# Attention on one Trainium2 core: softmax denominators by ones in both column halves, the output scaled on the vector engine, and one maxima piece between two score groups

## The reference, cut to what matters

```python
q = jnp.einsum('bnsd,neod->bneso', sx, wq)          # 4 heads x 4 experts
k = jnp.einsum('bnsd,nod->bnso', sx, wk)
v = jnp.einsum('bnsd,nod->bnso', sx, wv)
scores = jnp.einsum('bnesd,bntd->bnest', q, k) * d ** 0.5 + causal
att = jax.nn.softmax(scores, axis=-1)
qkv = jnp.einsum('bnest,bntd->bnesd', att, v)
qkv = jnp.where(pad[:, :, None], 0.0, qkv)
out = jnp.transpose(qkv, (0, 1, 3, 2, 4)).reshape(b, nh, s, ne * d)
gs = jax.nn.softmax(jnp.einsum('bnsf,nef->bnse', out, gate_w) + gate_b[None, :, None, :], axis=-1)
mixed = jnp.einsum('bnsed,bnse->bnsd', out.reshape(b, nh, s, ne, d), gs)
```

## Time and profile before

| | |
|---|---|
| median of 3 runs | 3468.97 us (3467.27 to 3474.9) |
| the profiled execution | 3469.29 us, span 3467.6 us |
| busy share of the span | PE 89%, PEld 54%, DVE 51%, ACT 36%, POOL 54% |
| instructions | 46110 |
| mean granted clock of PE | 0.937 |

### The profile page before, as it was taken

How to read it: one execution, slowest core, us unless ns; L and a number is a source line. 1 busy time by engine, 2 the same in 40 slices (tenths; PEclk the granted TensorE clock), 3 DMA queues, 4 the chain that set the end, 5 groups by cost and what they waited for, 6 DMA issues and landing times. The chain is left out here.

```text
span 3467.6 us, 46110 instructions
## 1 busy us (share of the span) xinstructions
PE 3079.7 (89%) x18162; PEld 1862.0 (54%) x18162; DVE 1757.7 (51%) x2797; ACT 1236.7 (36%) x1637; POOL 1862.6 (54%) x992
## 2 busy tenths in 40 slices
PE   7999987689998889999999999788999999999943
PEld 3445656377875555555555555455555555555422
DVE  4522764487833455565555640155656565563056
ACT  2210320356531233334444344233343434434423
POOL 0000020333310356778788899546677879889924
PEclk9999888899998799999999999789999999999966
DMA  9951100399950000000000000000000000000001
GB/s 392 424 207 46 60 1 8 110 295 272 261 94 15 1 1 1 1 1 1 1 1 1 1 1 1 1 1 1 1 1 1 1 1 1 1 1 1 1 4 40
DMA packets 63748, 195.36 MB, mean 56 GB/s; under 512 B 8243, under 2 KB 25137, under 8 KB 53554
## 3 DMA queue, kind: packets, MB, share of 16 engines
q1 hardware_dynamic: 38786, 148.11, 11.1%
q0 software_dynamic: 24752, 44.31, 7.1%
HBM read 188.99 MB, written 3.41 MB: 55 GB/s over the span
## 5 line engine op out<-in xcount | busy, mean ns | idle before, releaser
L1866 POOL TENSOR_TENSOR at_acc<-at_acc,at_pt 128x1024 f32<-128x1024 f32 (+3 forms) x728 | 1556.9, 2139 | 277.9 <-ACT at_pt L1702 194.7
L1762 DVE TENSOR_REDUCE at_mx<-at_psR 128x2 f32<-128x1024 f32 (+3 forms) x784 | 858.6, 1112 | 854.2 <-PE at_psR L1593 539.4
L1702 ACT ACTIVATE at_pt<-at_psR 128x1024 f32<-128x1024 f32 (+3 forms) x784 | 731.1, 936 | 991.5 <-PE at_psR L1614 607.3
L1630 PE MATMUL at_psO<-at_pt,v 128*64 128x512 f32 (+3 forms) x3136 | 702.7, 569 | 15.8 <-DVE at_oT L1781 10.6
L1611 PE MATMUL at_psR<-at_qhi,at_klo 64*128 64x512 f32 (+3 forms) x1568 | 345.9, 436 | 58.7 <-ACT at_pt L1702 27.5
L1630 PEld LDWEIGHTS at_psO<-at_pt,v 128*64 128x64 f32 x3136 | 193.1, 138 | 338.2 <-issue 277.2
L1593 PE MATMUL at_psR<-at_khi,at_qhi 64*128 64x512 f32 (+3 forms) x1568 | 341.9, 430 | 33.7 <-ACT at_pt L1702 9.4
L1246 PE MATMUL ga_acc<-h,ga_ring 128*128 128x257 f32 (+1 forms) x1352 | 305.3, 386 | 29.8 <-ACT ga_ring L1140 26.3
L1611 PEld LDWEIGHTS at_psR<-at_qhi,at_klo 64*128 64x128 f32 x1568 | 152.1, 188 | 328.9 <-issue 306.2
L1611 PE MATMUL at_psR<-at_qlo,at_khi 64*128 64x512 f32 (+3 forms) x1568 | 300.8, 377 | 0.0
L1611 PE MATMUL at_psR<-at_qhi,at_khi 64*128 64x512 f32 (+3 forms) x1568 | 300.1, 376 | 0.0
(11 more groups left out here) (318 smaller groups left out, 3276.8 us busy)
## 6 DMA issues: line engine op xcount, KB each, us to landing
gc_rows<-in_adj SPq DMA_DIRECT2D x26, 1664.0 KB, 17.3
ga_rows<-in_adj SPq DMA_DIRECT2D x26, 1664.0 KB, 9.9
ga_ring<-in_adjT POOLq DMA_DIRECT2D x78, 512.0 KB, 23.7
gc_cols<-in_adjT SPq DMA_DIRECT2D x26, 1024.0 KB, 15.1
gc_ring<-in_adjT SPq DMA_DIRECT2D x26, 512.0 KB, 7.6
gc_ring<-in_adjT SPq DMA_DIRECT2D x13, 256.0 KB, 2.8
ga_ring<-in_adjT POOLq DMA_DIRECT2D x13, 256.0 KB, 9.2
out_x<-X SPq DMA_DIRECT2D x6, 512.0 KB
```

What stands on the lines that cost most here:

```text
L1630: ins = pe.matmul(psO[lanes[l], off:off + w], v1[:, t, (2 * hp + l) * D:(2 * hp + l + 1) * D], pt[:, g % PTS, l, 0:w], start=g == FIRST[u] ...
L1702: act.activation(pt[:, g % PTS, :, 0:w], psR[:, slot_of["score", g] % SLOTS, :, 0:w], ACT.Exp).then_inc(e_ready, 1)
L1762: dve.tensor_reduce(mx[:, u % 2, :, s, c:c + 1].rearrange("p l o -> p (l o)"), psR[:, slot_of["max", i] % SLOTS, :, 0:w], AX.X, ALU.max).t ...
L1866: pool.tensor_tensor(to, to, got, ALU.add).then_inc(added, 1)
```

## The change

The turn `t` no longer makes the denominators. A new turn `d` comes ahead of it: for each head one matmul with a 128x64 block of ones as stationary and all of `acc` (up to 512 columns) as moving operand, into the head's 64 partitions of `psX`, so that each denominator stands in 64 rows. `scale_out` on DVE takes the reciprocal in place in `psX` and multiplies `oT` by it. The turn `t` then waits for `o_scaled`. In a step list `d` stands where the first `t` stood (step 1), the two `t` stand one step later (steps 2 and 3, or the last step if there are fewer). The gate no longer divides. Its pieces come a step later in units of 5 or more steps, and in units of 5 steps pieces 1 and 2 fall into the same step. `max_pieces` keeps the number of pieces of a step but puts at most one after the first score group: (2,1) becomes (1,2), (3,3) becomes (1,5). POOL may start on a reused `acc` after `d` instead of after the last `t`.

```diff
@@ late_turns
-        out += [("t", u - 1, h) for h in range(halves_of(u - 1)) if k == min(1 + h, ls - 1)]
+        if k == min(1, ls - 1):
+            out.append(("d", u - 1))
+        out += [("t", u - 1, h) for h in range(halves_of(u - 1)) if k == min(2 + h, ls - 1)]
@@ max_pieces
-    lo, hi = (len(some) * (2 * k + h) // (2 * steps_of(u)) for h in (half, half + 1))
+    lo, hi = (len(some) * x // steps_of(u) for x in (k, k + 1))
+    between = min(lo + 1, hi)
+    lo, hi = (lo, between) if half == 0 else (between, hi)
@@ gate_pieces
-            return [(hp, b, i) for i in range(3) if k == 2 + i]
+            return [(hp, b, i) for i in range(3) if k == (3 + i if ls >= 6 else min(3 + i, 4))]
@@
-LAST_TURNS = [("t", NU - 1, h) for h in range(halves_of(NU - 1))]
+LAST_TURNS = [("d", NU - 1)] + [("t", NU - 1, h) for h in range(halves_of(NU - 1))]
@@ tensor
+                def denominators(u):
+                    bw = QBLOCKS[UNITS[u][1]][1]
+                    pe.wait_ge(x_read, turn_of["d", u])
+                    pe.wait_ge(added, FIRST[u + 1])
+                    for l in range(2):
+                        ins = pe.matmul(psX[lanes[l], 0:bw], ones_f[:, :], acc[:, u % 2, l, 0:bw], start=True, stop=True)
+                    ins.then_inc(x_full, 1)
+
                 def turn_out(u, h):
                     hp, b, e = UNITS[u]
                     pe.wait_ge(x_read, turn_of["t", u, h])
-                    pe.wait_ge(o_read, u + 1)
-                    pe.wait_ge(added, FIRST[u + 1])
+                    pe.wait_ge(o_scaled, u + 1)
                     for s in range(2 * h, 2 * h + 2):
-                        o = (s - 2 * h) * (TCOLS + 2)
-                        pe.matmul(psX[:, o:o + TCOLS], oT[:, u % 2, s * P:(s + 1) * P], tg_sb[:, hp, e, :],
-                                  start=True, stop=True)
-                        for l in range(2):
-                            ins = pe.matmul(psX[:, o + TCOLS + l:o + TCOLS + l + 1],
-                                            acc[:, u % 2, l, s * P:(s + 1) * P], one[:, :], start=True, stop=True)
+                        o = (s - 2 * h) * TCOLS
+                        ins = pe.matmul(psX[:, o:o + TCOLS], oT[:, u % 2, s * P:(s + 1) * P], tg_sb[:, hp, e, :],
+                                        start=True, stop=True)
                     ins.then_inc(x_full, 1)
@@ vector
+                def scale_out(u):
+                    bw = QBLOCKS[UNITS[u][1]][1]
+                    dve.wait_ge(x_full, turn_of["d", u] + 1)
+                    link(dve.reciprocal(psX[:, 0:bw], psX[:, 0:bw]))
+                    dve.wait_ge(o_read, u + 1)
+                    dve.tensor_tensor(oT[:, u % 2, 0:bw], oT[:, u % 2, 0:bw], psX[:, 0:bw], ALU.mult).then_inc(o_scaled, 1)
+                    dve.wait_ge(o_scaled, u + 1)
+                    dve.sem_inc(x_read, 1)
@@ vector, gate
-                        link(dve.reciprocal(rden[:, 0:ws, :, :].rearrange("p s e l -> p (s e) l"),
-                                            onx[:, 0:ws, :, 2 * NE:2 * NE + 2].rearrange("p s e l -> p (s e) l")))
-                        link(dve.tensor_tensor(
-                            gp[:, 0:ws, :, :].rearrange("p s e (l g) -> p (s e) l g", g=NE),
...
-                        link(dve.tensor_tensor(gates, gates, gate_max.unsqueeze(2).broadcast_to([P, 2 * ws, NE]), ALU.mult))
-                        dve.tensor_tensor(wgt[:, 0:ws, :, :], gs[:, 0:ws, :].rearrange("p s (l g) -> p s g l", l=2),
-                                          rden[:, 0:ws, :, :], ALU.mult).then_inc(gate_ready, 1)
+                        for l in range(2):
+                            ins = dve.tensor_tensor(
+                                wgt[:, 0:ws, :, l], gs[:, 0:ws, l * NE:(l + 1) * NE],
+                                gate_max.rearrange("p (s l) -> p s l", l=2)[:, :, l:l + 1].broadcast_to([P, ws, NE]), ALU.mult)
+                        ins.then_inc(gate_ready, 1)
@@ gpsimd, add_up
                         if u >= 2:
-                            pool.wait_ge(x_full, last_turn(u - 2) + 1)
+                            pool.wait_ge(x_full, turn_of["d", u - 2] + 1)
```

More of the change, by code:

```diff
@@ L1486, in stage_attention @@
         ones_r = m.sb("at_ones_r", [P, P], F32R)
-        one = m.sb("at_one", [P, 1])
+        ones_f = m.sb("at_ones_f", [P, D])
         pt = m.sb("at_pt", [P, PTS, 2, BLK])
@@ L1516, in stage_attention @@
         added = m.sem("at_added")
-        o_read = m.sem("at_o_read")
+        o_read, o_scaled = m.sem("at_o_read"), m.sem("at_o_scaled")
         gate_shifted, gate_exped, gate_ready = m.sem("at_gate_shifted"), m.sem("at_gate_exped"), m.sem("at_gate_ready")
@@ L1571, in turn_out @@
                     pe.wait_ge(x_read, turn_of["t", u, h])
[L1572 to L1573 removed]
+                    pe.wait_ge(o_scaled, u + 1)
                     for s in range(2 * h, 2 * h + 2):
[L1575 to L1580 removed]
+                        o = (s - 2 * h) * TCOLS
+                        ins = pe.matmul(psX[:, o:o + TCOLS], oT[:, u % 2, s * P:(s + 1) * P], tg_sb[:, hp, e, :],
+                                        start=True, stop=True)
                     ins.then_inc(x_full, 1)
                 def turn(kind, *what):
[L1584 removed]
+                    {"k": keys, "q": queries, "r": row_of_maxima, "d": denominators, "t": turn_out}[kind](*what)
                 def row_max(u, i, s, c, w):
@@ L1688, in turn_out @@
                         act.wait_ge(mix_done, block_number(hp, b))
-                    got = psX[:, 0:2 * (TCOLS + 2)].rearrange("p (s c) -> p s c", s=2)
+                    got = psX[:, 0:2 * TCOLS].rearrange("p (s c) -> p s c", s=2)
                     act.activation(on[:, 2 * h:2 * h + 2, e, :], got[:, :, 0:P], ACT.Copy)
-                    act.activation(onx[:, 2 * h:2 * h + 2, e, :], got[:, :, P:TCOLS + 2], ACT.Copy).then_inc(x_read, 1)
+                    act.activation(onx[:, 2 * h:2 * h + 2, e, :], got[:, :, P:TCOLS], ACT.Copy).then_inc(x_read, 1)
                 def turn(kind, *what):
-                    {"k": keys, "q": queries, "r": row_of_maxima, "t": turn_out}[kind](*what)
+                    if kind != "d":
+                        {"k": keys, "q": queries, "r": row_of_maxima, "t": turn_out}[kind](*what)
                 def exps(g):
@@ L1758, in turn @@
                         queries(*what)
+                    elif kind == "d":
+                        scale_out(*what)
                 def row_max(u, i, s, c, w):
@@ L1849, in _ @@
                         maxima(u + 2)
+                for x in LAST_TURNS:
+                    turn(*x)
                 for piece in range(3):
@@ L1878, in _ @@
                 pool.memset(ones_r[:, :].bitcast(F32), 1.0).then_inc(consts, 1)
-                pool.memset(one[:, :], 1.0).then_inc(consts, 1)
+                pool.memset(ones_f[:, :], 1.0).then_inc(consts, 1)
                 pool.memset(isel[:, :, :], 0.0).then_inc(hides, 1)
```

9 lines of the change are left out of this document (2 added, 7 removed).

## The result

The changed kernel takes 3482.9 us (median of 8 runs, 3476.42 to 3487.8) against 3469.17 us (8 runs, 3462.45 to 3474.9): a ratio of 1.004, 95% interval 1.0028 to 1.0051. It is slower by 13.7 us, where 25 had been forecast. The profiled execution took 3487.8 us, span 3486.1, which is 18.5 us over the span of before. It is the slowest of the eight, so its span overstates the loss by some 5 us.

The account below looks back on a forecast made before the run. PE was taken to bound the attention stage nearly everywhere. Terms of -25, -1, -16, +1, +28, +19, +4, +10, +3 and +2 sum to +25 us on 3469.3: 3494 us, range 3460 to 3520.

Parts of the forecast that it names:

- rival (a): DVE's reciprocal is cheap when wide, 0.69 us like its neighbours: 3449 us, faster; chance 0.08.
- PE's matmuls (-0.7 a unit): In 512-query units, `t` without ones and the new `d` save PE 0.7 us; -25 us over 36 units.
- Rival (e): PE's saving doesn't come, as changing to `d` costs more or loads don't pack: +15, 3509 us; chance 0.07.
- The order (-16): 36 steps change piece order; (2,1) to (1,2) saves 0.48 us of scores waiting for exponentials: -16 us.
- The late slots (+28): Long units: DVE's hold makes step 2's third maxima piece, or `t`, late: +28 us (10 to 40).
- Rival (c): `t` is late in every unit, reciprocal and semaphores dearer, 0.3 to 0.5 us in 36 units: 3508 us; chance 0.2.
- (b): Reciprocal as priced, the three slots absorb DVE's hold, only short units and gate pay: 3469 us, no change; chance 0.17.
- (d): Reciprocal has no fixed part, 3.9 us for 512 columns, every hold 0.6 us longer: 3524 us; chance 0.03.
- Short units (+19), 5 and 33 (+4): One-step units chain `d`, reciprocal, product, `t`, `q`: +19 us; units 5 and 33, DVE late out of a gate: +4.
- The clock's +2: PE stands still longer in short units and behind units 8 and 36, its granted clock lower: +2 us (0 to 8).
- The gate in the five-step units (+10): Units 8, 36: two gate pieces share the last step before `take_out`, 4.7 us more each; with 12, 40: +10.
- The gate in the long units: Piece 0 loses two DVE operations, gaining nothing since PE doesn't wait for DVE there; units 12, 40: +0.5 us each.

Follow-up runs that it names:

- experiment 3: Changed kernel with a plain copy in place of the reciprocal, so output is multiplied by the denominators: 3438.45 us, ratio 0.9917 to the kernel before.
- experiment 1: Kernel before with the new order of the maxima pieces alone: 3461.99 us, ratio 0.9979.
- experiment 9: Changed kernel with the value products ahead of `t` in one-step units: 3483.85 us, ratio 1.0054 to the kernel before.
- experiment 4: Changed kernel with the third gate piece of five-step units moved to step 0 of the next unit: 3472.38 us, ratio 1.0009 to the kernel before.
- experiment 5: Kernel before with the gate pieces one step later in blocks whose units have six or more steps: 3463.85 us, ratio 0.9985.
- Experiment 11: Changed kernel with gate pieces of units of six or more steps back at steps 2, 3 and 4: 3509.73 us, ratio 1.0116 to the kernel before.

## Why the prediction was right or wrong

**Right: sign, and the mechanism with its price.** The reciprocal's 3.30 us measured 3.36. By rival (a) a cheap one would give 45 us; experiment 3 gave 44.5, though its parts are other than forecast (below) and the clock has a share in it.

**PE's matmuls (-0.7 a unit).** Unit 51 is 1.71 us shorter in experiment 3 and 0.99 in experiment 1, so `d` and `t` without the ones give 0.72. Rival (e) is out. The value products of unit 22 in the changed kernel, for the earlier trace rows:

```profile
1863.03 0.50 PE L1599 MATMUL at_psR<-at_khi,at_qhi 64*128 64x512 f32 x2 [1.14 <-DVE at_mx L1780]
...
1864.12 1.94 PE L1636 MATMUL at_psO<-at_pt,v 128*64 128x512 f32 x8
...
1869.49 1.94 PE L1636 MATMUL at_psO<-at_pt,v 128*64 128x512 f32 x8
...
1874.20 1.94 PE L1636 MATMUL at_psO<-at_pt,v 128*64 128x512 f32 x8
...
1879.47 1.94 PE L1636 MATMUL at_psO<-at_pt,v 128*64 128x512 f32 x8
```

A (1,1) step with a `t` takes 5.37 us (1864.12 to 1869.49), 0.66 over the plain 4.71 behind it; 0.67 was forecast. The (1,2) step at the end takes 5.27 where (2,1) took 5.61: 0.34 less, 0.48 forecast.

**The order (-16).** In the changed kernel it is worth 16.6 us, 13.6 of them at the same mean clock. The forecast was right.

**The late slots (+28).** The third maxima product of step 2 waits 1.14 us for its slot in the rows above, in the range of 1.0 to 1.3. The slot waits grew by 22 us in all, not 25. By unit, against experiment 3 and at full clock in both: 1.2 us each in 18, 19, 22, 23 and their likes (1.1 forecast), 1.85 in 10, 11 and theirs (2.2), 0.4 in 14 and 15 (0.8), 0.5 in 6 and 7 (1.6). That is 21 us where 27 were forecast. (The prediction's 28 holds the 1 us for `t`, which its sum adds once more.) In the changed kernel's own profile units 38 and 39 cost more, and that is the clock: experiment 9 runs the same program in them. Unit 38 took 31.10 us at a clock of 0.95 and 29.53 at 1.00. Unit 39, first in the changed kernel, then in experiment 9 (length, busy us of PE, weight loads, DVE, ACT, POOL, granted clock):

```profile
2475.43:2508.02 32.59, 30.02 (x200) 15.94 (x198) 20.59 (x23) 11.09 (x16) 19.02 (x11) 0.90 0.00 1
```

```profile
2459.56:2489.09 29.53, 26.94 (x200) 14.74 (x198) 20.58 (x23) 11.09 (x16) 19.04 (x11) 1.00 0.00 1
```

**A just-in-time `t` in (1,1) steps (+1).** Of the 18 waits of `t`, nine are in units of one and three steps (1.4 to 4.3 us), one is at the end (4.27), four in units 14, 15, 42 and 43 (0.34 each, 0.8 forecast) and four in the units that POOL paces (0.52). The other long units have none. Rival (c) fell with that; so did (b), since the slots didn't absorb the hold, and (d) by the 3.36 us.

**Short units (+19), 5 and 33 (+4).** Units of one step are 21.5 us longer, 5 and 33 together 5.5. But experiment 3 leaves 13.8 of the 21.5: more than the reciprocal stood behind them, the handover from `d` over DVE to `t`, and the clock. In the profiled execution the stretch 1142 to 1245 us had 0.87 before and this after:

```profile
1142.00:1245.00 103.00, 80.68 (x551) 44.91 (x551) 59.67 (x93) 27.76 (x50) 35.44 (x24) 0.80 0.00 1
```

Over the span the mean clock fell from 0.937 to 0.932; at two levels, full and half, that is (1 - 0.937) x 2 x 3467.6 = 437 us at the lower one before and (1 - 0.932) x 2 x 3486.1 = 474 after. Those 37 us more cost at most 18, what full speed would save. **The clock's +2 was sized too low.** The fall isn't chance: the eight executions of the changed kernel lie at 0.931 to 0.933, all 75 of before at 0.935 to 0.942. By the 2.4 us for each 0.001 that the kernel before shows, the 0.006 between the medians is some 15 us, an estimate: as much as the whole change lost. In the profiled execution the one-step units have 25 us more at the lower level than before, the five-step units 34 more (units 38 and 39 above are two of them) and the first units of the long blocks 16 less. Which part of the change brings the clock down stays open; without the reciprocal (experiment 3) the median is 0.934.

**The gate in the five-step units (+10).** Units 8 and 36 grew by 5.2 us each, and experiment 4 took back 10.5, clock included.

**The gate in the long units: the step that failed.** The prediction put the two operations that piece 0 loses at nothing, since "DVE isn't what PE waits for at that point", and priced the gate at +0.5 in units 12 and 40. The first units of the long blocks (12, 16, 20, 24, 40, 44, 48, 52) came out 17.1 us shorter: 0.7 each, 5.6 in all, by PE's products; 6.5 by PE's waits, which fell from 28.9 to 22.4 us; the other 5 come with the clock. In unit 16 the two stalls behind the gate were 0.80 and 2.64 us before and are 0.28 and 1.85 now. The later step alone doesn't do that (experiment 5 has 31.7 us of waits). What does is seen in unit 44, which ran at full clock in both. First experiment 5, where the unit starts at 2628.88, then the changed kernel, from 2657.55:

```profile
2656.89 3.62 POOL L1873 TENSOR_TENSOR at_on<-at_on,at_wgt 128x2048 f32<-128x2048 f32 x1 [3.62 <-DVE at_wgt L1812]
...
2664.15 0.50 PE L1593 MATMUL at_psR<-at_khi,at_qhi 64*128 64x512 f32 x2 [1.43 <-ACT at_pt L1702]
```

```profile
2683.68 3.63 POOL L1888 TENSOR_TENSOR at_on<-at_on,at_wgt 128x2048 f32<-128x2048 f32 x1 [3.14 <-DVE at_wgt L1823]
...
2690.93 0.50 PE L1599 MATMUL at_psR<-at_khi,at_qhi 64*128 64x512 f32 x2 [0.25 <-ACT at_pt L1709]
```

POOL's product starts 28.0 us into the unit in the one and 26.1 in the other. ACT, which waits for POOL's additions behind it, waits 4.00 and 2.83 us, and PE for ACT 1.43 and 0.25. So PE did wait for DVE's gate pieces here, by way of POOL and ACT. Of the 1.9 us, 0.7 are PE's shorter products; 0.63 is the length of the two operations that piece 0 lost (0.34 and 0.29 in experiment 5). No run left out these two alone, so their share isn't shown. Experiment 11 shows that with the late `t` the step is needed: a step less costs 27 us.

**The end (+3).** Behind the last unit it is 1.5 us longer: `d` 1.97 us at the lower clock and PE's 4.27 us for DVE are nearly paid for by the shorter turns and gate.

**Luck.** The sum came near, 25 forecast against 13.7, though two misses in it are each about as large as the result: the clock cost some 13 us more than its +2, and the gate in the long units (7) and the late slots (6) together as much less than forecast. The one-step units, whose 21.5 us hold a part of the clock's, were sized somewhat too high as well.

## What to carry to other kernels

An engine that is free nearly half the time can still be the wrong place for a long operation when other engines wait for the short ones in its queue: put a price on what stands behind it, not on its busy time. Here the same inverse, 3.4 us on DVE or 3.7 on ACT with two table loads, differs by 20 us in the whole kernel by whose queue it blocks (9 to 16 at the same clock). When a producer is moved a step later, everything that consumes it in order has to move with it: one gate left a step too early costs 27 us, more than the whole change. Before an engine is said not to be waited for, follow the chain through the others: here DVE's gate reached PE by way of POOL and ACT. And set each run's granted clock beside its time, since experiment 5 gained 7 us with PE's waits no shorter in sum.

## What the runs showed of the hardware that wasn't expected

Table loads of 1.28 us, 112 of them, were mostly hidden: ACT's busy time in the stage from 1113 to 3300 us rose from 846 to 1048 us and the kernel became 20 us faster than with the reciprocal on DVE.

The same DVE addition of 128x512 in SBUF took 2.75 us at 1301.71 of the changed kernel, while POOL was working on `acc`, and 0.69 us at the end of the stage with POOL idle:

```profile
1299.08 7.58 POOL L1881 TENSOR_TENSOR at_acc<-at_acc,at_pt 128x1024 f32<-128x1024 f32 x3
...
3339.48 0.69 DVE L1832 TENSOR_TENSOR hn<-hn,at_mixed 128x512 f32<-128x512 f32 x1
```

POOL has no row in the trace at 3339.48. The two times were seen; that POOL's work is the reason is inferred from them.

TensorE's granted clock scatters from run to run in places where PE stands often. One program, that of experiment 9, took 3468.6 to 3504.7 us, which is more than the change it was to test. Nor is it only scatter: kernels whose medians are 7 us apart can differ by no more than their clock (experiment 5).
